# A layer with windowed attention and a feed-forward block: periods that open with complete scores, and the output projection a period later in another bank

## The reference

```
x1  = x  + attention(layernorm(x))      # 16 heads of 8, causal window of 32 tokens, then @ Wo + bo
out = x1 + ffn(layernorm(x1))
ffn(z): h = gelu(z @ (W1 + scale * M1).T + b1);  h @ (W2 + scale * M2).T + b2
```

## Time and profile before

| | |
|---|---|
| three executions | 123.05, 127.38, 128.72 us |
| profiled execution | 124.22 us, span 122.5 us |
| busy, share of the span | TensorE 83%, VectorE 63%, ScalarE 55%, GpSimd 54% |
| chain of work that ended last | TensorE 54%, VectorE 20%, GpSimd 7%, ScalarE 7%, issue 6%, DMA 3% |
| granted clock of TensorE, mean | 0.889 |
| first copy of the scores, chunks 0 to 7 | 12.59, 22.58, 30.32, 40.04, 49.35, 57.97, 68.34, 76.00 us |
| last product ends, last store lands | 119.75 us, 122.5 us |

### The profile page before, as it was taken

How to read it: one execution, slowest core, us unless ns; L and a number is a source line. 1 busy time by engine, 2 the same in 40 slices (tenths; PEclk the granted TensorE clock), 3 DMA queues, 4 the chain that set the end, 5 groups by cost and what they waited for, 6 DMA issues and landing times.

```text
span 122.5 us, 5472 instructions
## 1 busy us (share of the span) xinstructions
PE 101.6 (83%) x2374; PEld 79.6 (65%) x2374; DVE 77.3 (63%) x201; ACT 68.0 (55%) x132; POOL 66.2 (54%) x80
## 2 busy tenths in 40 slices
PE   6878669898965499797799895679989958999990
PEld 5846438787845388576698765553464944875990
DVE  1758694888795859799589499798360058320031
ACT  4722864875925587785698778760093904408000
POOL 7772549395639359499955299991097006000000
PEclk9999985559999779999558999855999999999999
DMA  3981121121210211221210121000000000202032
GB/s 93 274 256 49 31 40 51 29 51 35 50 45 0 32 40 32 38 51 24 37 49 4 28 53 32 0 8 0 0 5 0 5 0 0 86 0 86 0 93 83
DMA packets 13977, 5.48 MB, mean 45 GB/s; under 512 B 8448, under 2 KB 13824, under 8 KB 13952
## 3 DMA queue, kind: packets, MB, share of 16 engines
q1 hardware_dynamic: 13664, 4.92, 16.5%
q10 hardware_dynamic: 288, 0.20, 0.7%
HBM read 1.97 MB, written 1.05 MB: 25 GB/s over the span
## 4 chain that ended last, share of the span: by engine, by line
PE 54%; DVE 20%; POOL 7%; ACT 7%; issue 6%; DMA 3%; DVEq 0%; ACTq 0%
PE bank_s L422 13%; POOL sraw L197 7%; PE bank_s L338 6%; PE bank_p L436 6%; PE bank_o L378 5%; PE bank_o L359 4%; PE bank_t L436 4%; DVE rowmax L630 4%; DVE probsT L636 4%; PE bank_t L313 3%; ACT sraw L499 3%; PE bank_o L368 3%; DMA x_sb<-in_x 3%; DVE xn L617 2%; DVE att L643 2%
## 5 line engine op out<-in xcount | busy, mean ns | idle before, releaser
L197 POOL TENSOR_TENSOR sraw<-sraw,rowmax 128x512 f32<-128x512 f32 x32 | 32.6, 1043 | 16.0 <-DVE rowmax L630 16.0
L531 ACT ACTIVATE probs<-sraw 128x512 f32<-128x512 f32 x32 | 19.7, 633 | 11.1 <-POOL sraw L197 11.0
L636 DVE STREAM_TRANSPOSE probsT<-probs 128x512 f32<-128x512 f32 x32 | 20.9, 687 | 4.2 <-ACT probs L531 4.1
L630 DVE TENSOR_REDUCE rowmax<-sraw 128x8 f32<-128x512 f32 x32 | 20.3, 677 | 2.7 <-ACT sraw L499 2.6
L499 ACT ACTIVATE sraw<-bank_s 128x512 f32<-128x512 f32 x32 | 17.3, 598 | 5.9 <-PE bank_s L338 5.9
L422 PE MATMUL bank_s<-x2T,w_rest 128*128 128x512 f32 x32 | 16.6, 668 | 2.6 <-DVE x2T L681 1.8
L338 PEld LDWEIGHTS bank_s<-KT,QS 32*128 32x128 f32 x512 | 17.4, 204 | 1.7 <-issue 1.1
L338 PE MATMUL bank_s<-KT,QS 32*128 32x64 f32 x512 | 17.6, 287 | 0.8 <-issue 0.8
L549 ACT ACTIVATE hidden<-bank_s,cols 128x512 f32<-128x512 f32 x16 | 10.3, 689 | 9.8 <-PE bank_s L422 9.6
L359 PE MATMUL bank_o<-V,probsT 128*32 128x36 f32 x1016 | 14.1, 221 | 1.1 <-issue 1.1
L359 PEld LDWEIGHTS bank_o<-V,probsT 128*32 128x32 f32 x1016 | 12.9, 128 | 2.9 <-issue 2.4
(11 more groups left out here) (86 smaller groups left out, 149.5 us busy)
## 6 DMA issues: line engine op xcount, KB each, us to landing
V<-v_sb SPq DMA_DIRECT2D x32, 36.0 KB, 2.0
QS<-qT SPq DMA_DIRECT2D x28, 32.0 KB, 2.4
x_sb<-in_x SPq DMA_DIRECT2D x1, 768.0 KB, 6.3
out_dram<-y SPq DMA_DIRECT2D x3, 256.0 KB, 2.2
w_rest<-in_w_rest SPq DMA_DIRECT2D x1, 576.0 KB, 6.3
x_sb<-in_x SPq DMA_DIRECT2D x2, 128.0 KB, 3.1
out_dram<-y SPq DMA_DIRECT2D x2, 128.0 KB, 1.8
w_qkv<-in_w_qkv ACTq DMA_DIRECT2D x1, 192.0 KB, 2.7
```

The costliest lines, as they stand in the source:

```text
L197: nc.gpsimd.tensor_tensor(sraw[g][:], sraw[g][:], rowmax[g][:].unsqueeze(2).to_broadcast([P, BLOCKS, 2 * WIN]), ALU.subtract).then_inc(cen ...
L531: nc.scalar.activation(probs[g][:], sraw[g][:].rearrange("p j k -> p (j k)"), ACT.Exp, scale=float(HD) ** -0.5).then_inc(probs_done, 1)
L630: nc.vector.tensor_reduce(rowmax[g][:], sraw[g][:], AX.X, ALU.max).then_inc(max_done, 1)
L636: nc.vector.transpose(probsT[u % 8][:].rearrange("p j q -> p (j q)"), probs[g][:]).then_inc(probsT_done, 1)
```

## The change

What it does, part by part:

- **Periods.** The loop index becomes n. A period n opens when all scores of chunk n are there. ScalarE copies all four groups at once, then v and the turned x, then three exponentials, copy_attT(n-1), the fourth exponential, q and k of chunk n+2. `copy_qk` is split in `copy_q` and `copy_k`.
- **TensorE's order** in a period: project_v(n+1), turn_x(n+2), out_proj(n-2), values(n-1), project(n+2), turn_att(n-1), scores(n+1). So the scores of the next chunk come last, the values one step earlier against the scores, and the output projection one period later.
- **Banks.** out_proj of chunks 0 to 4 goes to q's half of `bank_p` instead of `bank_o`; project(n+2) waits for residual(n-2), which reads it. Chunk 1 is turned and projected in `bank_o[0]`, right behind chunk 0, before the scores of chunk 0. `turn_x` no longer waits for the copy of v; `project_v` and `copy_v` wait instead. The update of W1 moves to `bank_p`, that of W2 to `bank_t`.
- **VectorE's order:** row_max 0 and 1, residual(n-2), row_max 2 and 3, normalise(n-1), ln1_norm(n+4), the four turn_probs(n), ln2_stats(n-2), then the variances. At the start, ln1_var(4, 8), which waits for the third load of x, stands ahead of spread_q0.
- **GpSimd:** the four centre(n) in a row; the second layernorm's work of two tiles at a time behind them.
- **SyncE:** q's planes of chunk 1 first, then V of chunk n+1 ahead of q's planes of chunk n+2.
- **End:** up(0, ·) and up(1, ·) are threaded with the last turn_att, out_proj and values; down(0) comes after turn_x2(2).

```diff
 # SyncE
+            planes(1)
+            spread_v(0)
+            for c in range(1, NCH):
+                spread_v(c)
+                if c + 1 < NCH:
+                    planes(c + 1)
 ...
 # GpSimd
+            ln1_rstd(3, 4, 8)
+            ln1_rstd(4, 8, 12)
+            for n in range(NCH):
+                if n == 2:
+                    ln1_rstd(5, 12, 16)
+                centre(n, 0)
+                centre(n, 1)
+                centre(n, 2)
+                centre(n, 3)
 ...
+                if n in (4, 6):
+                    ln2_rstd((n - 4) // 2)
+                    ln2_norm((n - 4) // 2, 0, 2)
+                if n in (5, 7):
+                    ln2_norm((n - 5) // 2, 2, FT)
 ...
 # TensorE
             def project(c):
                 pe.wait_ge(xT_done, c + 1)
-                ge(pe, kT_done, c)
-                ge(pe, qT_done, c - 1)
+                if c >= 2:
+                    pe.wait_ge(kT_done, c)
+                    pe.wait_ge(qT_done, c - 1)
+                    ge(pe, x1_done, c - 3)
 ...
             def out_proj(c):
 ...
                 pe.wait_ge(attT_done, c + 1)
+                if c < 5:
+                    pe.wait_ge(kT_done, min(c + 4, NCH))
+                    to, at = bank_p, 0
+                else:
+                    to, at = bank_o[c % 2], CHUNK
 ...
             turn_x(0)
+            turn_x(1)
             pe.wait_ge(qkv_in, 16)
+            project(0)
+            project(1)
+            project_v(0)
+            pe.wait_ge(query_set, 1)
+            pe.wait_ge(mask_set, 2)
+            scores(0)
+            for n in range(NCH):
+                if n + 1 < NCH:
+                    project_v(n + 1)
+                if n + 2 < NCH:
+                    turn_x(n + 2)
+                if n >= 2:
+                    out_proj(n - 2)
+                if n == 5:
                     even_tokens()
+                if n >= 1:
+                    for g in range(NG):
+                        values(n - 1, g)
+                if n + 2 < NCH:
+                    project(n + 2)
+                if n == 6:
+                    update_w1()
                     turn_x2(0)
+                if n < LAST:
+                    if n >= 1:
+                        turn_att(n - 1)
+                    scores(n + 1)
+            up(0, 0)
+            up(0, 1)
+            turn_att(6)
+            up(0, 2)
+            up(0, 3)
+            turn_x2(1)
+            update_w2()
+            out_proj(6)
+            for g in range(NG):
+                values(7, g)
+            up(1, 0)
+            up(1, 1)
+            turn_att(7)
+            up(1, 2)
+            up(1, 3)
+            out_proj(7)
+            turn_x2(2)
             down(0)
-            out_proj(LAST)
-            turn_x2(2)
 ...
 # ScalarE
+            for n in range(NCH):
+                for g in range(NG):
+                    copy_scores(n, g)
+                if n + 1 < NCH:
+                    copy_v(n + 1)
+                if n + 2 < NCH:
+                    copy_xT(n + 2)
+                if n == 5:
                     act.wait_ge(even_ps, 1)
+                    act.wait_ge(x1_done, 4)
+                    ident_act(even[:], bank_p[:, CHUNK:CHUNK + D]).then_inc(even_done, 1)
+                for g in range(NG - 1):
+                    softmax_exp(n, g)
+                if n >= 1:
+                    copy_attT(n - 1)
+                softmax_exp(n, NG - 1)
+                if n + 2 < NCH:
+                    copy_q(n + 2)
+                    copy_k(n + 2)
+                if n == 5:
                     token_pairs(0, pair1)
+                if n == 6:
                     token_pairs(1, pair2)
 ...
 # VectorE
             dve.wait_ge(x_in[2], 16)
+            ln1_var(4, 8)
             dve.wait_ge(head_set, 1)
             dve.wait_ge(cols_done, 16)
             spread_q0()
+            ln1_norm(2)
+            ln1_norm(3)
+            ln1_var(8, 12)
+            for n in range(NCH):
+                row_max(n, 0)
+                row_max(n, 1)
+                if n >= 2:
+                    residual(n - 2)
+                row_max(n, 2)
+                row_max(n, 3)
+                if n >= 1:
+                    normalise(n - 1)
+                if n + 4 < NCH:
+                    ln1_norm(n + 4)
+                for g in range(NG):
+                    turn_probs(n, g)
+                if n == 1:
+                    ln1_var(12, 16)
+                if n >= 2:
+                    ln2_stats(n - 2)
+                if n in (3, 5, 7):
+                    ln2_var((n - 3) // 2)
+                if n == 6:
                     copy_x2T(0)
                     update_w1()
+            copy_x2T(1)
+            update_w2()
+            residual(6)
+            ln2_stats(6)
+            normalise(7)
+            residual(7)
+            ln2_stats(7)
             ln2_var(3)
             copy_x2T(2)
             ln2_norm(3)
```

More of the change, by code:

```diff
@@ L160, in _, with planes, spread_v @@
             sp.dma_start(w_rest[:], w_rest_in).then_inc(w_in, 16)
[L162 to L171, removed]
+            def planes(c):
+                sp.wait_ge(qT_done, c)
+                if c < 3:
+                    sp.wait_ge(QS_zero, c)
+                else:
+                    sp.wait_ge(s_ps, NG * (c - 2))
+                for h in range(GH):
+                    sp.dma_start(QS[c % 3][h::GH, :, h],
+                                 qT[c % 2][h::GH].rearrange("p (j q) -> p j q", q=WIN)).then_inc(QS_in[c % 3], 16)
+            def spread_v(c):
                 sp.wait_ge(v_done, c + 1)
@@ L214, in ln2_norm @@
                     pool.wait_ge(update_ps, 2)
-                for t in range(FT):
+                for t in range(t0, t1):
                     i = FT * f + t
@@ L249, in _ @@
                 nc.gpsimd.memset(V[b][:], 0.0).then_inc(V23_zero, 1)
[L250 to L258, removed]
+            ln1_rstd(3, 4, 8)
[7 more added lines that the diff above has]
+                centre(n, 3)
+                if n == 0:
                     pool.wait_ge(w_in, 16 * N_W)
[L260 to L262 removed]
+                if n < 4:
+                    add_bo(4 * n, 4 * (n + 1))
+                if n == 2:
                     nc.gpsimd.affine_select(out=shift[:], in_=ones[:], compare_op=ALU.is_equal, fill=0.0, base=1,
@@ L449, in _ @@
             turn_x(0)
+            turn_x(1)
             pe.wait_ge(qkv_in, 16)
-            for c in range(-2, NCH):
-                if c == -1:
-                    pe.wait_ge(query_set, 1)
-                    pe.wait_ge(mask_set, 2)
-                    scores(0)
-                if c + 2 < NCH:
-                    project(c + 2)
-                if 1 <= c + 1 < NCH:
-                    scores(c + 1)
-                if c >= 1:
-                    turn_att(c - 1)
-                if c + 2 < NCH:
-                    project_v(c + 2)
-                if c >= 1:
-                    out_proj(c - 1)
-                if c + 3 < NCH:
-                    turn_x(c + 3)
-                if c == 4:
-                    even_tokens()
-                for g in range(NG):
-                    if c >= 0:
-                        values(c, g)
-                if c == 4:
-                    turn_x2(0)
-                if c == 5:
-                    update_w1()
-                if c == 6:
-                    for i in range(HC):
-                        up(0, i)
-                    turn_x2(1)
-                    update_w2()
```

175 lines of the change are left out of this document (61 added, 114 removed).

## The result

The changed kernel takes 114.82 us in the median (113.38 to 115.86, four executions); the kernel before, run beside it, 125.22 us (122.92 to 128.72). The ratio is 0.923 with a 95% interval of 0.913 to 0.933. Executions of either kernel fall into faster and slower ones, and the ratio compares the faster ones alone, so it is not the quotient of the medians. The profiled execution took 115.86 us, the longest of the four; its span is 114.0.

What follows compares the result with a forecast made beforehand. No engine was full; round trips between engines and a falling clock lost the time. Chunk 7's first copy at 69.1 plus the end's 39.9 gave 109.0, plus 1.7 around it 110.7, plus a 3.3 clock spell 114.0 us; range 108.5 to 121.

Steps and rivals of the forecast that it cites:

- The end: From chunk 7's first score copy to the last store: 39.9 us against 46.50 before.
- The period's four chains: Steady attention period: the chains of TensorE, VectorE, GpSimd and ScalarE steps all close at 6.9 to 7.0 us.
- the sum: Start, seven periods and end added up: span 109.0 us, execution 110.7 us, before the added clock spell.
- TensorE alone would need 6.9 us: Steady period: TensorE's steps, added by their lengths from project_v to scores, take 6.9 us.
- the order has no slack there: Slower rival: at the lower clock TensorE's steps form one chain of 11.1 us a period; 132.8 us, chance 0.05.
- one more spell of the lower clock: One whole period at the lower clock costs TensorE 11.1 us against 7.8, so 3.3 us is added.
- It recovered within two slices each time: Argument against the slower rival (chance 0.05): in the earlier profile the lowered clock rose again within two slices.
- ln1_norm beside the subtraction: Periods 1 to 3: VectorE's moved ln1_norm is held up by GpSimd's fourth subtraction, 0.9 us a period, 2.7 altogether.
- The planes' cover: q's planes land 0.8 us before the scores want them; a landing of 3.5 us would show 0.3 a period.
- The start: ln1_var(4, 8) waits for the third load, delaying spread_q0; chunk 0's scores ready at 13.5 us instead of 12.59.
- Marks set beforehand: Signs for right or wrong: score copy distances, ln1_norm's length, waits of VectorE, GpSimd, TensorE and copy_attT, clock, end under 41 us.
- the rival in which periods stay as they were: A new wait replaces the old, periods stay at 9.06 us, only the end gains: 118.5 us, 121.8 with a spell; chance 0.18.

Runs made afterwards that it cites:

- second trace: The changed kernel, unaltered, traced again in an execution of 113.41 us; its end takes 39.54 us.
- With the supply mostly out of the way: Changed kernel with project_v as two whole 128x256 products instead of 32 of 32 columns (v not the reference's): 110.29 us, ratio 0.892.
- the executions at the same clock: Clock 1.00 throughout: changed kernel with out_proj back in bank_o, 111.66 us; changed kernel with project_v as two whole products, 108.28 and 109.40 us.
- the kernel with the old end: Changed kernel with TensorE's end unthreaded again (up(0) whole before turn_att(6), down(0) before out_proj(7) and turn_x2(2)): 117.24 us, ratio 0.953.
- with bf16: Changed kernel with probabilities and V in bf16 and ln1_norm behind the turns: 108.52 us, ratio 0.869; with out_proj also back in bank_o: 108.06 us.

## Why the prediction was right, and where it was not

**The end: right.** 39.9 us forecast, 39.49 measured, and the steps lie near where they were put: down(0) ends at 93.2, 18.7 us after chunk 7's first copy (19.1 forecast). The old order gives 43.48.

**The period's four chains: right as a floor, wrong as what binds.** From chunk 0's first copy to chunk 7's the sum had 69.1 - 13.5 = 55.6 us without the clock. With the supply mostly out of the way and the clock up it is 53.85, with periods down to 6.72 us. The changed kernel itself took 60.52 (58.11 in its second trace). The step of the prediction that failed is "TensorE alone would need 6.9 us": that counts the lengths of its instructions and not that they must be supplied. The same holds for "the order has no slack there": it looked only at the clock.

**The term of 3.3 us for one more spell of the lower clock: about the right size, with a term beside it missing.** The loop took 60.52 - 55.6 = 4.9 us more than the sum had without the clock. Of the 6.7 us above 53.85, the supply is 2.3 to 3.4 and the clock 3.3 to 4.4, by the estimate from the executions at the same clock; the supply's part has no term in the sum, and the sum was 1.8 too long without it. That the two errors nearly cancel is luck. "It recovered within two slices each time" misreads: the first spell covers more than three slices.

What makes the clock fall stays open. In the changed kernel it fell within about 2.5 us of the end of TensorE's rests at 14.6 to 17.1 (two, with work between), 24.1 to 25.7, 42.4 to 44.4 and 54.9 to 56.0 us. But the kernel with the old end stood for 8.1 us in front of products of `values` and had a mean of 0.97 over its periods, and with bf16 the clock fell three times in a kernel whose stands are 1.1 us in all. So the stands in the supply by themselves do not decide it.

**ln1_norm beside the subtraction: the mechanism right, its price not on the path.** The pairs of periods 0 to 3 took 1.51, 1.92, 1.32 and 0.59 us; 0.9 a period was taken, 0.95, 1.36, 0.76 and 0.03 came. But moving it back gave nothing (0.926 against 0.923 and 0.928), so its 2.7 us do not belong in the changed kernel's sum. With fewer instructions they may: there the four pairs took 6.6 us, and VectorE was busy for 8.86 of the 8.96 us of period 2. That was not tested by itself. In exchange the variance steps took 0.17 us each where one had taken 0.85. The Trainium skill's rule ("SBUF — State Buffer", Who interferes with whom), that a VectorE tensor_scalar in a two-port mode and a GpSimd instruction exclude each other, agrees with these lengths. Whether the hold-up matters it does not say; that the timing decides.

**The planes' cover: thin, as said, and twice too thin.** TensorE waited 1.0 and 0.2 us for QS. The longer wait in order of time, and the time to landing of the QS DMAs between 40 and 80 us:

```profile
55.96 2.01 PE L350 MATMUL bank_s<-KT,QS 32*128 32x64 f32 x64 [1.02 <-DMA QS<-qT]
```

```profile
DMA to landing us min/median/max: 1.9/2.6/3.8
```

One landing took 3.8 us, where 3.5 had been put as the bad case.

**The start: right size, wrong holder.** 13.99 us against 13.5. spread_q0 began at 9.37, as forecast (9.6), and ended before it was needed. TensorE was the last: the two projections and project_v(0) ended at 11.79.

```profile
9.37 1.90 DVE L659 TENSOR_SCALAR QS<-bank_o,cols,head_of 128x256 f32<-128x256 f32 x4
...
11.03 0.76 PE L325 MATMUL bank_t<-w_qkv,xT 128*32 128x32 f32 x64
```

**Marks set beforehand that failed.** First score copies were to be 7 to 8.5 us apart from chunk 2 on; two of the five distances are longer, 10.88 and 8.83, and chunk 7's came at 74.51 instead of near 69. GpSimd's wait for maxima was to be below 8 us and is 15.6: its subtractions are in one row now, and the wait lies between periods. copy_attT waited over 1 us for turn_att, with the exponential behind it, in period 3. All of them belong to the rival in which periods stay as they were; that rival had 0.18 and was closer to the loop (9.06 to 8.65 us a period) than the forecast was, though the new wait that it names is not the one that came. The total came out right because the start was little off and the end right, and by luck in the loop, where a cost that was not foreseen met a sum that was too long.

## What to carry to other kernels

Count TensorE's instructions a period, not only their time. Where many small products are packed behind one another, look for "issue" in front of a product in the midst of equal ones, and for equal distances between such places. Taking rests out of TensorE's order can turn them into waits for its own program; then the next gain is fewer instructions (one pass instead of two, wider products), and an edit that is worth nothing in the old order can be worth 3 to 6% in the new one.

## What the runs showed of the hardware that was not expected

- TensorE's stands recur at a distance of 256 instructions or multiples of it (weight loads and matmuls each count one; a float32 product of `values` counts two of each, a bf16 one). The instruction queue moved 19, 15 and 23 DMAs for 4813, 3853 and 5837 of TensorE's instructions. In all traces 89 such stands end 2.2 to 3.0 us after the start of a DMA of that queue, which started after the block before was entered (0.8 to 2.5 us after it for the stands of the changed kernel).
- Doubling one step's small products, with 4.7 us more of busy time, made seven periods 11.0 us longer.
- In the feed-forward block a spell of the lower clock of 3.4 us costs about 1.7 us (46.50 us with 6.8 us of it, 44.78 with 3.4).
- A VectorE TENSOR_SCALAR of 0.34 us took up to 1.31 us beside GpSimd's TENSOR_TENSOR.
- VectorE's 32x32 turns take the same time in bf16 (692 ns) as in float32 (687 ns).
